# Attention rows spilled from the SP queue, and one sparse phase's results written by VectorE

## What is computed

```
x = x + 0.5 * ffn(layernorm(x))     # first:  c = 0
x = x + sparse(layernorm(x))        # the sparse attention
x = x + 0.5 * ffn(layernorm(x))     # second: c = 1, same weights

ffn:    dense causal attention, 16 heads of 8; layernorm; softmax gate, top 2 of 8 experts,
        gelu(h w1 + b1) w2 + b2 weighted and summed; layernorm
sparse: an indexer scores all keys for each query; the 64 latest keys and the best 32 others
        (96 in all) are gathered; attention of 8 heads over them, from a latent of 32;
        out = attended @ (W_uv W_out)
```

## Time and profile before

| | |
|---|---|
| time, median of 3 runs | 1666.84 us (1666.38 to 1671.42) |
| the profiled execution, its own time | 1667.76 us |
| its span in the profile | 1666.0 us |
| TensorE matmuls busy | 1392.9 us, 84% |
| VectorE busy | 1235.5 us, 74% |
| ScalarE busy | 980.9 us, 59% |
| GpSimd busy | 463.5 us, 28% |
| mean granted clock of TensorE | 0.914 of full |
| moved by DMA | 99.53 MB, 65147 packets |
| chain that ended last | PE 54%, DVE 12%, ACT 10%, issue 6%, SPq 6%, DMA 4%, DVEq 4% |

### The profile page before, as it was taken

The page is one execution under the profiler, slowest core; times in us unless marked ns, Lnnn a source line. Parts: engine busy times, 40 slices in busy tenths (PEclk is TensorE's granted clock), DMA queues, the critical chain, the costliest instruction groups (busy, mean ns, idle before and its releaser), DMA issues.

```text
span 1666.0 us, 31709 instructions
## 1 busy us (share of the span) xinstructions
PE 1392.9 (84%) x10630; PEld 911.5 (55%) x10664; DVE 1235.5 (74%) x2552; ACT 980.9 (59%) x1792; POOL 463.5 (28%) x755
## 2 busy tenths in 40 slices
PE   5699999799994843899898998995599999799994
PEld 3355554577773311556565655674355555577773
DVE  5578885697778586777888887754578887588787
ACT  2366666578882583346556545553166666488883
POOL 4122322100002037345555545623022233100000
PEclk9699999899997865899999999997599999799998
DMA  5311110022202236022132112211611110022200
GB/s 158 85 45 47 47 48 4 1 103 76 76 26 79 51 87 160 21 57 65 38 82 68 47 54 62 76 35 21 170 44 40 43 48 18 1 103 76 76 26 25
DMA packets 65147, 99.53 MB, mean 60 GB/s; under 512 B 21283, under 2 KB 45027, under 8 KB 62966
## 3 DMA queue, kind: packets, MB, share of 16 engines
q1 hardware_dynamic: 53142, 71.84, 15.0%
q0 software_dynamic: 8192, 16.79, 4.0%
q10 hardware_dynamic: 3680, 9.19, 1.7%
HBM read 69.00 MB, written 10.69 MB: 48 GB/s over the span
## 4 chain that ended last, share of the span: by engine, by line
PE 54%; DVE 12%; ACT 10%; issue 6%; SPq 6%; DMA 4%; DVEq 4%; POOL 1%; ACTq 1%; POOLq 0%
PE twin L1030 9%; PE twin L1020 5%; PE twin L882 5%; PE twin L1199 5%; PE twin L860 5%; PE twin L827 4%; DMA ffn<-arena 4%; ACT arena L1266 3%; SPq L484 3%; DVEq L1897 3%; ACT experts L1359 2%; PE twin L1227 2%; PE twin L1215 2%; PE twin L1180 2%; ACT arena L1357 2%
## 5 line engine op out<-in xcount | busy, mean ns | idle before, releaser
L1266 ACT ACTIVATE arena<-twin 128x1024 f32<-128x1024 f32 x288 | 294.1, 1024 | 165.9 <-PE twin L860 164.1
L783 POOL DMA_INDIRECT arena<-kv_rows,IDX x256 | 250.9, 980 | 214.5 <-PE twin L1246 144.9
L1560 DVE TENSOR_REDUCE arena<-twin 128x8 f32<-128x1024 f32 (+1 forms) x160 | 195.4, 1225 | 67.6 <-PE twin L827 33.2
L1357 ACT ACTIVATE arena<-twin,bias 128x512 f32<-128x512 f32 x256 | 185.1, 723 | 60.4 <-PE twin L1020 60.3
L1609 DVE TENSOR_TENSOR experts<-arena,experts 128x512 fp32r<-128x512 f32 x256 | 170.1, 689 | 61.7 <-ACT experts L1359 60.0
L1020 PE MATMUL twin<-experts,experts 128*128 128x512 f32 x768 | 197.4, 403 | 5.9 <-ACT experts L1359 5.8
L827 PE MATMUL twin<-ffn,ffn 64*128 64x128 f32 (+3 forms) x1152 | 154.7, 351 | 44.5 <-DMA ffn<-ffn 24.1
L743 POOL TENSOR_SCALAR_AFFINE_SELECT arena<-arena 128x256 f32<-128x256 f32 x256 | 99.6, 407 | 317.9 <-ACT arena L1266 317.9
L1550 DVE TENSOR_REDUCE arena<-twin 128x2 f32<-128x1024 f32 x128 | 153.1, 1222 | 47.1 <-PE twin L827 43.8
L1359 ACT ACTIVATE experts<-twin,bias 128x512 fp32r<-128x512 f32 x256 | 186.5, 728 | 0.0
L1030 PE MATMUL twin<-experts,experts 128*128 128x512 f32 x768 | 183.1, 390 | 1.0 <-DVE experts L1609 1.0
(11 more groups left out here) (260 smaller groups left out, 2187.3 us busy)
## 6 DMA issues: line engine op xcount, KB each, us to landing
arena<-wt_rows SPq DMA_DIRECT2D x16, 1024.0 KB, 5.0
arena<-in_L_ffn_w SPq DMA_DIRECT2D x32, 256.0 KB, 5.3
XT<-idx_rows SPq DMA_DIRECT2D x16, 512.0 KB, 4.6
ffn<-q_rows SPq DMA_DIRECT2D x48, 128.0 KB
ffn<-k_rows SPq DMA_DIRECT2D x48, 128.0 KB
ffn<-ffn SPq DMA_DIRECT2D x64, 64.0 KB
q_rows<-ffn ACTq DMA_DIRECT2D x8, 512.0 KB, 7.4
k_rows<-ffn ACTq DMA_DIRECT2D x4, 1024.0 KB, 13.8
```

The costliest lines, as they stand in the source:

```text
L783: pool.indirect_dma_start(G[d % GR][:, g, :], None, kv_rows, bass.IndirectOffsetOnAxis(ap=IDX[:, q, k * GB + g:k * GB + g + 1], axis=0))\
L1266: act.activation(PT[(UNITS * buf + u) % PT_RING].rearrange("p s n -> p (s n)"), twin[2 * u % S_RING][:, :], ACT.Exp, scale=float(HD) ** -0 ...
L1357: act.activation(H1[tb % 2][:, f, :], bank[f][:, :], ACT.Gelu_apprx_tanh, bias=bias1[buf][:, f:f + 1])
L1560: dve.tensor_reduce(to, scores.rearrange("p (s t k) -> p s t k", s=2, t=to.shape[2]), AX_X, ALU.max).then_inc(max_done, 1)
```

## The change

The spill's code moves from ScalarE's stream to SP's (`sp_spill`), without a change in its six copies. In the SP queue it stands behind the rows and values of pair 3. The wait for rows_spilled moves into `sp_rows`, in front of each load of rows. In the second stage the weights of experts 0 and 1 are issued after the loop, behind the rows of pair 15 and ahead of the maxima of pair 13. In the sparse part the last phase (7) no longer goes through `sp_moved`: `dve_attended` writes its four groups directly to OAX, each of its two copies replaced by four of 32 partitions x 64 elements, one for each partition group. TensorE waits for the other phases' copies and for the count of all groups before the second batch's tokens.

```diff
--- before.py
+++ after.py
@@ -501,6 +501,8 @@
 
         def sp_rows(sp, c, it, buf):
 
+            for b in range(B):
+                sp.wait_ge(rows_spilled[b], (PARTS + 1) * 16 * (c + 1))
             sp.wait_ge(pv_done, PV0 + len(GROUPS) * (PAIRS * c + it - RING + 1))
             pair = bass.ds(it, 1)
             for s in range(2):
@@ -519,6 +521,13 @@
                 r, j = TILE * s + PRODS, s * MAXROWS * TB
                 sp.dma_start(QB[buf][r:r + MAXROWS, :].bitcast(F32).rearrange("r (t q) -> r t q", q=P),
                              MT[j:j + MAXROWS * TB, :]).then_inc(maxrow_loaded, 16)
+
+        def sp_spill(sp, c, b):
+            sp.wait_ge(low_done, 8 * c + 8 // B * (b + 1))
+            pairs, t = slice(b * (PAIRS // B), (b + 1) * (PAIRS // B)), slice(b * L, (b + 1) * L)
+            for r in range(PARTS):
+                sp.dma_start(q_rows[pairs, :, r].rearrange("j s d t -> (j s) d t"), qparts[:, r, t].bitcast(F32)).then_inc(rows_spilled[b], 16)
+            sp.dma_start(k_rows[pairs].rearrange("j s d r t -> (j s d) r t"), kparts[:, :, t].bitcast(F32)).then_inc(rows_spilled[b], 16)
 
         def sp_expert(sp, c, e, buf):
             if not isinstance(e, int):
@@ -551,15 +560,15 @@
             sp_maxrows(sp, c, 0, 0)
             sp_first(sp, c, 3, rows_loaded[3])
             sp_values(sp, 3, 3)
-            if c:
-                for e in range(2):
-                    sp_expert(sp, c, e, e)
             for b in range(B):
-                sp.wait_ge(rows_spilled[b], (PARTS + 1) * 16 * (c + 1))
+                sp_spill(sp, c, b)
             with sp.Fori(1, PAIRS // RING) as i:
                 for k in range(RING):
                     sp_maxrows(sp, c, i * RING + k - (RING - 1), (k + 1) % RING)
                     sp_rows(sp, c, i * RING + k, k)
+            if c:
+                for e in range(2):
+                    sp_expert(sp, c, e, e)
             for it in range(PAIRS - RING + 1, PAIRS):
                 sp_maxrows(sp, c, it, it % RING)
             if c == 0:
@@ -664,7 +673,7 @@
             for q in range(5, PHASES):
                 sp_near(sp, q)
             sp.wait_ge(ix_done, SCORED[-1] + 1)
-            for q in range(4, PHASES):
+            for q in range(4, PHASES - 1):
                 sp_moved(sp, q)
 
         def pool_rstd(pool, n):
@@ -1132,8 +1141,11 @@
                 pe_mixed(pe, i)
 
             for gq in range(NG):
-                if gq % (NG // B) == 0:
-                    pe.wait_ge(oa_moved[gq // (NG // B)], 16 * NH * TB)
+                if gq == 0:
+                    pe.wait_ge(oa_moved[0], 16 * NH * TB)
+                elif gq == NG // B:
+                    pe.wait_ge(oa_moved[1], 16 * NH * (TB - 2))
+                    pe.wait_ge(oa_ready, NB // 4)
                 for t in range(4):
                     tile = 4 * gq + t
                     for x in range(NH * DC // P):
@@ -1302,15 +1314,6 @@
                 m = act.activation(KB[0][r, :], neghalf[r, 0:1].broadcast_to([ROWS - PRODS, L]), ACT.Copy, scale=-2.0)
             m.then_inc(first_filled, 1)
 
-        def act_spill(act, c):
-
-            for b in range(B):
-                act.wait_ge(low_done, 8 * c + 8 // B * (b + 1))
-                pairs, t = slice(b * (PAIRS // B), (b + 1) * (PAIRS // B)), slice(b * L, (b + 1) * L)
-                for r in range(PARTS):
-                    act.dma_start(q_rows[pairs, :, r].rearrange("j s d t -> (j s) d t"), qparts[:, r, t].bitcast(F32)).then_inc(rows_spilled[b], 16)
-                act.dma_start(k_rows[pairs].rearrange("j s d r t -> (j s d) r t"), kparts[:, :, t].bitcast(F32)).then_inc(rows_spilled[b], 16)
-
         def act_ffn(act, c):
             n_turn = (0, 4)[c]
             if c:
@@ -1328,7 +1331,6 @@
                     dst = VA[:, b * (PAIRS // B):(b + 1) * (PAIRS // B), :, t0 + t, 0:HD].rearrange("p a s d -> p (a s) d")
                     m = act.activation(dst, bank[g][:, t * P:(t + 1) * P].rearrange("p (h d) -> p h d", d=HD), ACT.Copy)
                 m.then_inc(va_ready, 1)
-            act_spill(act, c)
             act_maxrow(act, c, 0)
             for u in range(HALFWAY):
                 act_exp(act, c, 0, 0, u)
@@ -1982,6 +1984,11 @@
                 _, _, tile, k = place(4 * j + 2 * pair)
                 t0 = tile * P + k * BT
                 cols = slice(pair * 2 * P, (pair + 1) * 2 * P)
+                if 4 * j >= PER * (PHASES - 1):
+                    heads = o[:, cols].rearrange("p (g x r t) -> p r x g t", x=2, r=4, t=4)
+                    for r in range(4):
+                        m = dve.tensor_copy(OAX[r * DC:(r + 1) * DC, :, t0:t0 + 2 * BT].rearrange("p x (g t) -> p x g t", t=4), heads[:, r])
+                    continue
                 m = dve.tensor_copy(OA[:, :, t0:t0 + 2 * BT].rearrange("p h (g t) -> p g h t", t=4),
                                     o[:, cols].rearrange("p (g h t) -> p g h t", h=NH, t=4))
             m.then_inc(oa_ready, 1)
```

## The result

After the change the kernel takes 1659.6 us, the median of 10 runs (1650.2 to 1672.1); the kernel before took 1667.8 us beside it (10 runs). The ratio is 0.9946, 95% interval 0.9922 to 0.9970: 9.0 us faster, 5 to 13. The forecast was 1647 us, 20 us faster. The measured time lies inside the range, at its very end; the gain is less than half of the forecast.

What follows compares the result with a forecast made beforehand. TensorE's matmuls were taken to carry most of the chain. Gains of 10.6 us (sparse part), 4.6 (first attention) and 4.7 (second) made 19.9 off the profiled 1667.76; adjusted to the median, 1647 us, range 1635 to 1660.

Steps and rivals of the forecast that it cites:

- turn of the first maxima: Start of the first attention: TensorE turns pair 0's maxima at 48.1 us in place of 55.8, without the spill beside the loads.
- hold at pair 1: End of each attention's first step: pair 1's maxima wait behind the spill in the SP queue, 3.3 and 3.7 us.
- clock after that pause: Step after the wait at the second pair's scores: TensorE at its lower clock, 2.0 us each, bounds 0 and 3.1.
- mixing, first to last: End of the sparse part: the 8.35 us wait goes and the second half keeps its clock, 10.9 us gained.
- longer copies of the last phase: Sparse part: three more groups get longer VectorE copies while blocks still run, charged 0.3 us, bounds 0 and 6.9.
- T: Each attention: time from the spill's first issue to the landing of the maxima behind it, taken as 15.5 us.
- The formula: First attention's hand-over to pair 1: delay is 5.5 + 15.5 - 17.7 = 3.3 us.
- the first rival: Spill not in the way: small copies overtake it or it ends by T = 12; 30.9 us gained, 1636; chance 0.26.
- The start costs more than it gives: Slower case, start of the attentions: maxima land later still and the start loses from T = 17; chance 0.04.
- Nothing, 0 to 1: Second attention: expert weights moved behind pair 15's rows, landing near 1386.2 like pair 13's maxima before; cost nothing, 0 to 1.
- late maxima of pair 13: Second attention: pair 13's maxima arriving late would show the forecast wrong; no size given.
- Part 1: End of the sparse part: VectorE writes the last phase in place of 16 SP copies, 10.6 us gained.

Runs made afterwards that it cites:

- the run that mends it: The changed kernel with the second attention's four weight copies behind pair 15's maxima; 0.9918 (0.9893 to 0.9942) against the kernel before.
- the kernel without part 1: The changed kernel with the spill halved and the weights last, phase 7 as in the kernel before; 0.9881 (0.9852 to 0.9911) against the kernel before.

## Why the forecast was too high

Step by step, in the forecast's order; measured numbers are of the kernel after, and of its second profile where a second one stands behind "or".

| term | forecast | measured |
|---|---|---|
| turn of the first maxima; first scores | 48.1; 51.9 us | 47.34; 51.12 |
| spill starts; pair 1's maxima landed | 57.4; 72.9 | 56.72; 73.06 |
| hold at pair 1, first and second attention | 3.3, 3.7 us | 4.2, 4.0 or 4.0, 4.4 |
| clock after that pause | 2.0 each | 5.2, 3.6 or 5.1, 1.2 |
| weights moved | 0 | 2.2 + 3.7 = 5.9 or 2.3 + 5.1 = 7.4 |
| mixing, first to last | gain 10.9 | 8.6, or 11.2 at full clock |
| longer copies of the last phase | 0.3 | 1.2 to 2.4 |

**What was right.** The start of each attention gave what it was to give, and for the reason named: loads without the spill beside them, VectorE as the next limit. The new wait was where it was said, within 1 us, and T was 16.3 us, near the 15.5 taken. The formula holds with the measured numbers: 5.6 + 16.3 - 17.7 = 4.2. The experiments show its cause. With half the spill ahead of the maxima the wait is gone. Behind all of it in one queue the last of the 48 rows moved only as the spill ended, and beside it in another queue all moved in its midst. That is the Trainium skill's rule (*DMA: Bandwidth & Descriptors*, "Queues, rings and completion order"), that an engine takes one queue's descriptors in order and turns only between queues; the forecast set it beside the sum as speaking against the change, and these two traces agree. The small copies don't overtake, so the first rival falls. How the 6.3 us divide between order and load stays open: the load alone took 6.0 at another moment.

Two sums of the forecast are off. The start costs more than it gives from T = 19 and not from 17 (20.3 - 6.2 = 2(T - 12)), and the turn of the first maxima adds up to 48.0. Neither moves the forecast.

**The step that failed most: "Nothing, 0 to 1"** for the weights. I compared the landing of the weights with the landing that pair 13's maxima had before, found them equal (1386.2 both), and took equal for free. But the maxima have to land behind the weights in the same queue, and this hand-over, like the others, has no slack: 1 MB put just ahead of it must show. I had written exactly this argument for the spill, two paragraphs above, and not used it here. It costs 4.0 us by the trace of that edit alone (5.2 by its times, which don't exclude nothing), 5.9 to 7.4 us by the two traces of the change, and at most about 9 by the run that mends it, whose clock after the first pause was also the better one. The forecast named late maxima of pair 13 as a sign that it was wrong, and they were late.

**The clock was under-charged.** I took 2.0 us for the step after a pause, with an upper bound of 3.1 from a first step. A first step runs at the lower level for part of its length only (0.69 in the mean of 52:69 above); the second step of the first attention ran at 0.52 for 14 us and lost 5.2. Three pauses were made (the weights' is the third) and charged twice: 4.0 us in the sum, 12.5 in the kernel after and 11.4 in its second profile. What a pause costs is not fixed: the same step took 19.7, 19.8 and 15.9 us in three runs whose first steps were 21.7 to 21.9 us long. Whether work put into the pause would save the clock wasn't tried.

**Part 1 was worth 5.7 to 6.6 us, not 10.6** (the interval of the edit alone is 1.8 to 9.5). The wait went as forecast. The second half's full clock came in 2 of the 8 profiles with this edit (7.4 us for all 64 matmuls); the other six took 9.0 to 9.9. TensorE still stands still for 0.6 to 0.8 us three times in the last groups, and in these it is granted less than full afterwards; that these small pauses are the cause was only argued. And the eight copies of 32x64 take 1.86 and 1.91 us a group, 0.23 each, where 0.18 was taken from a row of another shape. The last three groups take 27.8 to 28.6 us in place of 26.2 to 26.6. In the trace's chain VectorE's copies stand ahead of the ScalarE work for which TensorE waits there, so the "gaps" of VectorE did not hide all of them.

**The sum, put right.** First attention 0.8 to 4.4 us of gain (0.8 in the kernel after, 9.7 - 4.0 - 1.3 with the weights last). In the second, from the first copy of its rows to the first scores, the kernel after takes 11.1 us less, so it loses about 2 (11.1 - 4.0 - 3.6 - 5.9, and 11.1 - 4.4 - 1.2 - 7.4 in its second profile). Part 1 gives 6 to 9. Together 4 to 11 us, against 9.0 on the first chip and 5.5 on the second. The halved spill puts the two attentions right: 28 us for the whole, of which some 21 are the attentions' (the kernel without part 1). That the pauses and their slow steps made the difference is seen in the first two steps of both attentions, 79.2 us with the weights last and 64.0 with the spill halved: 15.2 us, where the two kernels' times differ by 9 to 13.

## What to carry to other kernels

A queue's order is part of a transfer's latency: a small copy on which the next step hangs moves behind the bytes already in its queue, though its own issue was on time and the issuing engine free. Beside bulk in another queue it moves in its turn, but not for nothing (6.0 us to landing in place of 3.2). So put bulk behind it, or halve the bulk around it, and when you price such a move, check every hand-over of the queue that the moved bytes now stand ahead of, by landing and not by issue. Where TensorE is the bound, price a delay of 2 to 5 us as a range: with the step at the lower clock that follows it cost 1.3 to 3 times its length in these runs. Look first for a version that makes no stall.

## What the hardware showed that was not expected

- After a pause of 4.3 us TensorE had 0.52 of its clock for 14 us of nearly full work in one execution, and after one of 5.4 us 0.80 over 10 us in another. This may be part of the spread of the runs after (1650 to 1672 us), where those of the kernel before beside them lay within 10.5 (1661.5 to 1672.0); of the ten runs after, the fastest had a mean clock of 0.919 and the slowest 0.903.
- The spill moved faster alone: 4.19 MB between 56.7 and 72.2 us, 0.38 MB a us at the best, against 22 us beside the pair loads. The issues slowed with each further copy: 1.88 us for the first two of 512 KB and 3.05 for the last two, 1.55 and 2.76 us for the two of 1 MB, and 2.52 us for the two small ones behind in place of 1.64.
- 1 MB of weights, all issued by 1375.07, still held copies issued at 1377.71 until 1383.00. An idle issuing queue doesn't mean an empty one.
